# Additive attention on one core: GpSimd takes the fourth strip of every other full step, the gates' exponent is issued three steps later, and diagonal steps start at their own key

## What is computed

```python
f = x @ W1[:h];  g = x @ W1[h:]                       # 16 hidden units a token
t = tanh(f[:, :, None, :] + g[:, None, :, :] + b1)    # every query with every key
scores = t @ w2 + b2
e = exp(scores) * strictly_lower_triangle
w = e / (e.sum(-1) + 1e-10)
x = x + w @ x_normed
x = x + sum over the two best of 8 experts of p * (x_normed @ expert_w + expert_b)
```

## Time and profile before

| what | value |
|---|---|
| median of three runs | 7100.1 us |
| the profiled execution | 7095.91 us, span 7094.1 us |
| this stage | from 2890 to 7045 us of the span |
| busy in the whole span | PE 81%, DVE 84%, ACT 73%, POOL 19% |

### The profile page before, as it was taken

One profiled execution on the slowest core, in us unless ns is written; L12 is line 12 of the kernel. 1 busy time (PEld: TensorE's weight loads), 2 busy tenths in 40 slices (PEclk: granted clock), 3 DMA queues, 4 the chain that ended last, 5 costly groups with the idle time before them and its releaser, 6 DMA issues. The chain is left out here.

```text
span 7094.1 us, 89115 instructions
## 1 busy us (share of the span) xinstructions
PE 5769.6 (81%) x32962; PEld 2052.8 (29%) x32962; DVE 5925.0 (84%) x13228; ACT 5182.1 (73%) x3342; POOL 1334.8 (19%) x1463
## 2 busy tenths in 40 slices
PE   7887886788759998778888778888788887788887
PEld 2222222344324443222222222222222222222222
DVE  6888887676557774889999889999899998899997
ACT  3333322455545553799999999899999999999997
POOL 4444442000125663200001000001000000000000
PEclk8888887888869998899999999999999999999998
DMA  3111100101000000000000000000000000000000
GB/s 123 54 46 47 51 23 8 30 22 25 18 9 1 1 1 4 7 1 1 1 1 1 1 1 1 1 1 1 13 1 1 1 1 13 1 1 1 1 13 13
DMA packets 44444, 95.23 MB, mean 13 GB/s; under 512 B 7783, under 2 KB 9577, under 8 KB 42730
## 3 DMA queue, kind: packets, MB, share of 16 engines
q1 hardware_dynamic: 43114, 88.44, 3.8%
q0 software_dynamic: 896, 1.06, 0.1%
HBM read 39.14 MB, written 33.55 MB: 10 GB/s over the span
## 5 line engine op out<-in xcount | busy, mean ns | idle before, releaser
L2874 ACT ACTIVATE aa_tanh<-aa_tanh 128x4096 f32<-128x4096 f32 (+5 forms) x1120 | 3671.6, 3348 | 35.4 <-DVE aa_tanh L3055 35.0
L3055 DVE TENSOR_SCALAR aa_tanh<-aa_f_times,aa_g_bias 128x1024 f32<-128x1024 f32 (+18 forms) x5120 | 3043.9, 643 | 230.2 <-PE aa_scores L2921 221.1
L2921 PE MATMUL aa_scores<-aa_tanh,consts_sb 128*32 128x512 f32 (+8 forms) x18432 | 2161.8, 584 | 382.3 <-ACT aa_tanh L2874 380.4
L2921 PEld LDWEIGHTS aa_scores<-aa_tanh,consts_sb 128*32 128x32 f32 x18432 | 598.3, 113 | 1743.4 <-issue 1100.0
L2846 POOL TENSOR_SCALAR aa_group_normed<-x_rows,norm_scale,aa_shift_plus 128x128 f32<-128x128 f32 x216 | 173.0, 812 | 3542.5 <-PE aa_turned L2962 3332.5
L2935 PE MATMUL aa_out_sum<-aa_weights,aa_normed 128*128 128x512 f32 (+3 forms) x1152 | 639.2, 638 | 96.7 <-DVE aa_weights L3064 91.2
L3165 DVE SCALAR_TENSOR_TENSOR x_rows<-aa_turned,consts_sb,x_rows 128x128 f32<-128x128 f32 x1728 | 594.8, 344 | 0.0
L860 PE MATMUL near_weights_spread<-near_tap_weights,near_spread_consts 36*64 36x512 f32 x3200 | 430.1, 650 | 68.0 <-DVE near_weighted L507 56.0
L2086 PE MATMUL qa_out<-qa_hidden_rows,qa_weights_in 128*128 128x512 f32 x1024 | 475.4, 608 | 0.0
L880 PE MATMUL near_out_sum<-near_weighted,near_w_out 128*128 128x512 f32 x576 | 356.3, 751 | 102.4 <-DVE near_weighted L507 102.4
L496 DVE TENSOR_TENSOR near_weights_spread<-near_weights_spread,near_values 128x1024 f32<-128x1024 f32 x256 | 313.9, 1226 | 119.3 <-PE near_weights_spread L860 118.9
(11 more groups left out here) (434 smaller groups left out, 6440.7 us busy)
## 6 DMA issues: line engine op xcount, KB each, us to landing
near_offsets<-near_offset_staged SPq DMA_DIRECT2D x45, 512.0 KB, 3.0
l_taps<-l_scan_in_out SPq DMA_DIRECT2D x256, 64.0 KB, 2.0
x_rows<-in_x SPq DMA_DIRECT2D x4, 2048.0 KB, 15.4
near_offset_y<-near_offsets SPq DMA_DIRECT2D x15, 512.0 KB, 4.0
near_offset_x<-near_offsets SPq DMA_DIRECT2D x15, 512.0 KB, 4.6
near_mask<-near_offsets SPq DMA_DIRECT2D x15, 512.0 KB, 5.3
out_x<-x_rows SPq DMA_DIRECT2D x3, 2048.0 KB, 6.3
out_x<-x_rows SPq DMA_DIRECT2D x1, 1536.0 KB, 5.0
```

The costliest lines, as they stand in the source:

```text
L2874: a.activation(TH[:, u % PLACES, 0:length], TH[:, u % PLACES, 0:length], ACT.Tanh).then_inc(th_ready, 1)
L2921: last = t.matmul(sp_[32 * q:32 * q + 32, n % 2, s:e], W2S[:, tt, :], TH[:, p, o + s:o + e], start=tt == 0, stop=tt == 3, tile_position=(0 ...
L3055: ins = v.tensor_scalar(TH[:, p, at[q]:at[q] + w - s], FR[:, m % 2, lo + s:CHUNK], GB[:, key:key + 1], None, ALU.add)
```

## The change

Three things are changed.

1. At full tiles the steps tt = 0 and tt = 2 become **shared** (384 places). DVE fills strips 0 to 2 and signals; POOL fills strip 3, in its own queue at that place, after the same `th_used` wait; ACT's tanh waits for both (`strip_ready`).
2. The gates' exponent moves from offset p + 8 to p + 11, and DVE's last two lots of the gating from p + 9 and p + 10 to p + 11 and p + 12.
3. At diagonal tiles strip q of step tt starts at query 32 q + 8 tt instead of 32 q (`key_row`), so that steps 1 to 3 are 8, 16 and 24 columns a strip narrower.

```diff
+        def key_row(n, q, tt):
+            return (32 * q + 8 * tt) * shape(n)[2]
+        def runs(n, tt):
+            return [shape(n)[4] - key_row(n, q, tt) for q in range(4)]
+        shared = [u for u, (n, some) in enumerate(places) if not shape(n)[2] and some[0] % 2 == 0]
...
-                for o, steps in (..., (9, range(12, 15)), (10, range(15, STEPS))):
+                for o, steps in (..., (11, range(12, 15)), (12, range(15, STEPS))):
-                raise_gates[at[p + 8]] = G
+                raise_gates[at[p + 11]] = G
...
             for u, (n, some) in enumerate(places):            # POOL
+                if u in shared:
+                    tt = some[0]
+                    last, used = places[u - PLACES]
+                    pool.wait_ge(th_used, 1 + 4 * last + used[-1] + 1)
...
+                    key, (p, at) = 16 * j + 12 + tt, place(n, tt)
+                    pool.tensor_scalar(TH[:, p, at[3]:at[3] + CHUNK], FR[:, m % 2, :], GB[:, key:key + 1], None, ALU.add).then_inc(strip_ready, 1)
                 if m + 1 < NM and i == (m % NCH + 1) * CT_ - 8 and some[0] == 0:
                     normalize(m + 1)
                 if u in normed_at:
                     normalize_group(normed_at[u], u)
...
                 a.wait_ge(sum_ready, 1 + u + 1)                # ACT
+                if u in shared:
+                    a.wait_ge(strip_ready, 1 + shared.index(u) + 1)
...
                 for q in range(4):                             # DVE, fill
-                    s = 32 * q * diagonal
+                    s = key_row(n, q, tt)
+                    if q == 3 and u in shared:
+                        if E is not None:
+                            add_expert(E, q)
+                        continue
-                    if q == 3 and tt == places[u][1][-1]:
+                    if q == (2 if u in shared else 3) and tt == places[u][1][-1]:
                         ins.then_inc(sum_ready, 1)
```

More of the change, by code:

```diff
@@ L2649, in attention_and_experts @@
         bank_full, bank_free = [sem(f"bank{i}_full") for i in range(2)], [sem(f"bank{i}_free") for i in range(2)]
-        (loaded_e, centring, mu_ready, sh_ready, gate_step, diff_ready, raised, sum_step, group_stats, sent) = (sem(n) for n in (
-            "experts_loaded", "centring_ready", "group_normed", "shift_ready", "gate_step", "gate_diff", "gate_exp", "expert_sum", "group_stats", "sent"))
+        (loaded_e, centring, mu_ready, sh_ready, gate_step, diff_ready, raised, sum_step, group_stats, strip_ready, sent) = (sem(n) for n in (
+            "experts_loaded", "centring_ready", "group_normed", "shift_ready", "gate_step", "gate_diff", "gate_exp", "expert_sum", "group_stats", "strip_ready", "sent"))
         NM = NB * NCH
@@ L2678, in shape @@
             return m, j, dg >= 0, max(dg, 0) * P, CHUNK - max(dg, 0) * P
-        def runs_at(w, diagonal):
-            widths = [w - 32 * q * diagonal for q in range(4)]
-            return [sum(widths[:q]) for q in range(4)], sum(widths)
+        def key_row(n, q, tt):
+            return (32 * q + 8 * tt) * shape(n)[2]
+        def runs(n, tt):
+            return [shape(n)[4] - key_row(n, q, tt) for q in range(4)]
         def in_a_place(n):
@@ L2693, in place @@
         def place(n, tt):
-            m, j, diagonal, lo, w = shape(n)
-            starts, length = runs_at(w, diagonal)
             u = place_of[n, tt]
-            return u % PLACES, [(tt - places[u][1][0]) * length + s for s in starts]
+            before = sum(sum(runs(n, k)) for k in range(places[u][1][0], tt))
+            return u % PLACES, [before + sum(runs(n, tt)[:q]) for q in range(4)]
+        shared = [u for u, (n, some) in enumerate(places) if not shape(n)[2] and some[0] % 2 == 0]
         def exponents_behind(n):
@@ L2755, in attention_and_experts @@
                     stats_at[place_of[at[p + 2 * PERIOD - 1]] + PLACES + 3] = G
-                for o, steps in ((4, range(0, 4)), (5, range(4, 8)), (6, range(8, 12)), (9, range(12, 15)), (10, range(15, STEPS))):
+                for o, steps in ((4, range(0, 4)), (5, range(4, 8)), (6, range(8, 12)), (11, range(12, 15)), (12, range(15, STEPS))):
                     choose[at[p + o]] = (G, steps)
-                raise_gates[at[p + 8]] = G
+                raise_gates[at[p + 11]] = G
                 G += 1
@@ L2851, in _ @@
             for u, (n, some) in enumerate(places):
-                m = tiles[n][0]
+                m, j = tiles[n]
                 i = n - first_of[m]
+                if u in shared:
+                    tt = some[0]
+                    last, used = places[u - PLACES]
+                    pool.wait_ge(th_used, 1 + 4 * last + used[-1] + 1)
+                    if j == 0 and tt == 0:
+                        for name in ("f0", "f1", "g"):
+                            pool.wait_ge(*free(name, m))
+                    key, (p, at) = 16 * j + 12 + tt, place(n, tt)
+                    pool.tensor_scalar(TH[:, p, at[3]:at[3] + CHUNK], FR[:, m % 2, :], GB[:, key:key + 1], None, ALU.add).then_inc(strip_ready, 1)
                 if m + 1 < NM and i == (m % NCH + 1) * CT_ - 8 and some[0] == 0:
@@ L2871, in _ @@
                 m, j, diagonal, lo, w = shape(n)
-                length = len(some) * runs_at(w, diagonal)[1]
+                length = sum(sum(runs(n, tt)) for tt in some)
                 a.wait_ge(sum_ready, 1 + u + 1)
+                if u in shared:
+                    a.wait_ge(strip_ready, 1 + shared.index(u) + 1)
                 a.activation(TH[:, u % PLACES, 0:length], TH[:, u % PLACES, 0:length], ACT.Tanh).then_inc(th_ready, 1)
@@ L2918, in scores @@
                     for q in range(4):
-                        s, e = max(h, 32 * q * diagonal), min(w, h + BANK)
-                        o = at[q] - 32 * q * diagonal
+                        s, e = max(h, key_row(n, q, tt)), min(w, h + BANK)
+                        o = at[q] - key_row(n, q, tt)
                         last = t.matmul(sp_[32 * q:32 * q + 32, n % 2, s:e], W2S[:, tt, :], TH[:, p, o + s:o + e], start=tt == 0, stop=tt == 3, tile_position=(0, 32 * q))
```

## The result

The changed kernel takes **7560.4 us** (median of four runs, 7549.7 to 7565.4) against 7098.3 for the kernel before in the same comparison: a ratio of **1.065, 95% interval 1.064 to 1.067**, or 462 us more. Slower was forecast, at 7300 and with a range up to 7470: the direction was right and the size less than half of what came.

A forecast was written before the change was run, and what follows sets the result against it. ACT was taken to set the pace, with 204 us idle in 4145. Standing 274 plus DVE 72, less exponent 122 and diagonal 20, gave +204 on 7095.9: 7300 us, range 7150 to 7470.

The forecast's parts named there:

- the queue: POOL's strips queue behind its group normalization, which waits for PE's turn: 19 x 8.7 plus 19 x 5.7, 274 us of ACT standing.
- the strip's price: One fourth strip of 1024 columns on POOL was taken at 1.5 us, the middle between 0.66 and 2.37.
- DVE's term: POOL's strips hold DVE for 399 us against 254 saved; half of the 145 net on the path, 72 us.
- the exponent's wait: ACT's wait before the gates' exponent for DVE's twelfth gating operation, 122 us, goes in full when the exponent moves later.
- the twelve that were taken at nothing: Of POOL's 50 waits, 12 have the next shared place three or more places on; priced at no loss.
- The diagonal: Narrower steps at 128 diagonal tiles leave out 24,576 columns of tanh at 0.83 ns, saving ACT 20 us.
- The second: Rival: POOL's strip costs 2.37 us like a two-input operation and DVE is bound; +403, 7499 us; chance 0.13.
- The first: Rival: ACT's standing for POOL's strips is short, 155 us, and the change comes out even or faster, 7020; chance 0.12.
- The third: Rival: POOL is also late behind the 15 chunks it normalizes between strips; +75 us, 7375; chance 0.15.
- The fourth: Rival: DVE, held up by POOL, is still behind at p + 11, so the 122 us stay; 7422; chance 0.05.

## Why the prediction was right and where it failed

By the runs, taken in this order, the 462 us are 236 for the queue (the change against the one with the group later), 252 for the hold on DVE (that one against the one without strips on POOL) and -26 for the two other edits. I had 274, 72 and -142. Three steps failed: the strip's price, DVE's term, of which half of the net was put on the path, and the exponent's wait, which was to go in full. The missing time lies in the last two, and both rest on ACT setting the pace everywhere.

- **The queue: right in kind and in place; near in the sum (274 against 236) only because two errors offset.** ACT's new wait stands where it was put, in the places directly behind and next but one behind the 50 waits of POOL, 19 and 19 of them; they hold 19 x 14.0 + 19 x 10.0 = 456 of the 479 us, and the twelve that were taken at nothing hold 11. Taking the waits away by moving the group shows that 236 of it is the queue's own (248 with strips of 128 columns). In the trace the pieces are 14.0 and 10.0 us in the mean and not 8.7 and 5.7. Two terms of the piece were too small: the strip (2.8 to 3.0 there instead of 1.5), and POOL's start, 8.4 and 3.4 us after ACT was ready in the mean instead of 4.4 and 0.7, because PE itself runs behind when DVE is late with the experts' sums, as in the wait shown above. Against them stands what ACT would have waited for DVE anyway: with the group later 199 us come back in the waits for sums and scores.
- **The price of the strip: failed.** I took 1.5, between 0.66 and 2.37. It is 2.83 at least, outside both ends. The upper end was the wrong row: a two-input operation of the same width. The row of POOL's own tensor_scalar, 0.43 at 128 columns, was there; eight times that is 3.4, and 2.83 / 0.44 is 6.4. I explained that row away with a start-up read off another operation. By the Trainium skill's line-rate ("GPSIMD Engine Reference", engine selection) the strip was an estimated 1.2 us; the measured 2.83 decides. With 2.83 in its place the prediction's own sum would have been about 7606, and that this is near 7560 supports nothing: it needs 910 us of hold on DVE and 142 us of gains, and neither was there.
- **DVE: its place on the path failed, and the hold's size was luck.** I expected 399 us of hold on DVE, 145 net, and put half of the net on the path, 72 us, on the ground that ACT stands anyway. With the group later DVE is busy 262 us longer net, and the run is 252 us longer: as much as the whole net stands on the path. The run without fourth strips shows that DVE bounds the experts' stretches: 254 us off DVE give 118, and POOL's hold turns this gain into a loss of 252. The 399 lie near the 425 that DVE's full strips alone show, 2704 x (904 - 747) ns, because two errors offset: I took a strip of 1.5 us that holds DVE but for 0.46 us; the strip is 2.83 us and longer and holds DVE for a part of it (last section).
- **The exponent: failed, and for the same reason.** "The wait goes in full" was 122 us; 18 were measured. The wait went, and 100 us of it came back in the waits for scores and sums. The text had named the sums as what could be late next, priced that at nothing, and had not named the scores.
- **The diagonal: right in size**, 14 of 20.
- **The rivals.** The second had the place of the missing time, a dear strip with DVE as the bound, at 7499 with 0.13. The first, a short standing of 155 us, is refuted: even at 128 columns the queue alone keeps ACT for 245 us. The third, POOL late behind its chunks, was priced at 75 us; five of ACT's waits stand behind chunks, 13 us in all. The fourth had the exponent's gain missing, but not for its reason: it is missing without POOL's strips too.

My reading of the first view was the root of two failures. ACT 95% busy and DVE 92% over the whole stage does not say that ACT sets the pace everywhere; in the stretches with experts it was DVE. The wait before the exponent was the sign of it, and I took it for a fault of its own.

## What to carry to other kernels

A wait that an engine with nothing to do could sit through at no cost becomes a bound when awaited work is put behind it in the same queue: look at what already stands in that queue, and move the old wait behind the new work or the new work in front of it. Price an operation on another engine from that engine's own row of the same operation, scaled by its columns, before any other row. And when a stall is removed on the engine that seems to bound, ask what it was late for: if the other engine is behind in that stretch, the stall only moves to its next meeting.

## What the runs showed of the hardware that was not expected

**POOL's one-input operation is dearer than its two-input one.** 1024 columns of tensor_scalar with a column as the operand take 2.83 us (32 of the 384 strips ran with DVE silent throughout, and none of them took less), tensor_tensor 2.37 in the mean.

**POOL holds DVE in pieces, not for its whole operation.** While POOL made one strip from 5041.15 to 5044.37 and the next from 5044.36, DVE's timeline read (one narrow window each):

```profile
5041.15 3.22 POOL L2866 TENSOR_SCALAR aa_tanh<-aa_f_times,aa_g_bias 128x1024 f32<-128x1024 f32 x1
5041.19 1.09 DVE L3161 TENSOR_SCALAR aa_pick<-aa_max 128x4 f32<-128x4 f32 x1
...
5042.73 0.75 DVE L3074 TENSOR_SCALAR aa_tanh<-aa_f_times,aa_g_bias 128x1024 f32<-128x1024 f32 x1
```
```profile
5043.40 1.52 DVE L3074 TENSOR_SCALAR aa_tanh<-aa_f_times,aa_g_bias 128x1024 f32<-128x1024 f32 x1
```

A full DVE strip of 0.75 us, its own time, runs in the middle of POOL's strip, and the next takes 1.52; an operation of four columns takes 1.09 us (0.16 in the kernel before). So in these two DVE is kept for some 0.8 to 0.9 us at a time. The Trainium skill ("SBUF — State Buffer", who interferes with whom) says that, with DVE in one of its two-port modes, which tensor_scalar can enter, whichever of the two issues first keeps the shared pair for its whole instruction and blocks the other fully. For POOL against DVE these rows do not agree, and the measurement decides. What in POOL's operation sets the pieces was not tried.

**When ACT stands, PE stands too, and its granted clock falls.** Three stretches of the changed kernel, before a stand, in it and after it (the granted clock is the third number from the end):

```profile
7132.00:7140.00 8.00, 7.62 (x49) 2.09 (x42) 7.96 (x19) 0.59 (x2) 0.00 (x0) 1.00 0.00 0
7140.00:7149.00 9.00, 0.37 (x4) 0.13 (x2) 4.52 (x12) 3.02 (x1) 8.16 (x6) 0.65 0.00 0
7149.00:7154.00 5.00, 4.26 (x18) 1.17 (x19) 0.66 (x2) 5.00 (x3) 0.00 (x0) 0.61 0.01 3
```
```profile
7149.74 3.46 PE L2936 MATMUL aa_scores<-aa_tanh,consts_sb 128*32 128x512 f32 x16 [9.38 <-ACT aa_tanh L2889]
```

The granted clock is 1.00 (2.4 GHz) before the stand, 0.65 in the mean of the stretch with the stand and 0.61 after it, 0.50 being the lower level of 1.2 GHz. PE had stood for 9.4 us, and its first scores take 3.46 us where they took 1.92; behind its stand of 5.00 us in the timeline further up they take 3.64. What this adds to the time was not measured by itself; ACT's next tanh, 3.6 us, runs beside these scores.
